# Late input's statistics and normalising moved behind chunk masks, feed-forward steps placed between the products of an inversion, and one reload issued later

## What is computed

```
x = x + 0.5 * _L0_ffn_ref(_layernorm(x), gate, up, down)
x = x + _L0_attn_ref(_layernorm(x), ...)      # causal convs, gated delta-rule recurrence, 16 heads
x = x + 0.5 * _L0_ffn_ref(_layernorm(x), gate, up, down)
x = x + 0.5 * _L1_ffn_ref(_layernorm(x), W_r, W_k, W_v, mu_r, mu_k)
x = x + _L1_attn_ref(_layernorm(x), Wqkv, Wout)   # softmax inside blocks of 64
x = x + 0.5 * _L1_ffn_ref(_layernorm(x), W_r, W_k, W_v, mu_r, mu_k)
```

## Time and profile before

| | us |
|---|---|
| median of three runs | 8338.34 |
| lowest and highest | 8326.64, 8341.58 |
| span of the profiled execution | 8338.4 |
| PE busy | 6513.2 (78%) |
| DVE busy | 4672.6 (56%) |
| ACT busy | 2618.7 (31%) |
| POOL busy | 2154.0 (26%) |
| mean share of the full TensorE clock that was granted | 0.886 |

### The profile page before, as it was taken

The page is one execution under the profiler, slowest core; times in us unless marked ns, Lnnn a source line. Parts: engine busy times, 40 slices in busy tenths (PEclk is TensorE's granted clock), DMA queues, the critical chain, the costliest instruction groups (busy, mean ns, idle before and its releaser), DMA issues. The chain is left out here.

```text
span 8338.4 us, 162585 instructions
## 1 busy us (share of the span) xinstructions
PE 6513.2 (78%) x60160; PEld 4694.8 (56%) x60160; DVE 4672.6 (56%) x10226; ACT 2618.7 (31%) x5275; POOL 2154.0 (26%) x3555
## 2 busy tenths in 40 slices
PE   6787787877878788787877878778787787878776
PEld 4555646556565565655556465565655656556564
DVE  6556564554655546565464655546555465654653
ACT  3223242332423224242242423324233242422421
POOL 1413223041321413214032230413204132140321
PEclk9898898988989899898888989889888988988887
DMA  1100011001100110001100010010101110010000
GB/s 52 24 34 20 26 29 32 26 20 36 27 23 26 29 37 20 21 31 24 37 20 26 29 32 26 20 36 27 24 26 25 40 20 21 31 24 37 20 26 3
DMA packets 376529, 226.31 MB, mean 27 GB/s; under 512 B 336896, under 2 KB 353920, under 8 KB 367488
## 3 DMA queue, kind: packets, MB, share of 16 engines
q1 hardware_dynamic: 375680, 215.29, 9.4%
HBM read 156.54 MB, written 58.72 MB: 26 GB/s over the span
## 5 line engine op out<-in xcount | busy, mean ns | idle before, releaser
L806 DVE SCALAR_TENSOR_TENSOR PS<-SC,CW,PS 128x512 f32<-128x512 f32 x1536 | 1155.2, 753 | 157.7 <-DVEq L804 79.4
L1525 PE MATMUL PS<-CST,SC 128*128 128x128 f32 x2512 | 452.3, 322 | 462.9 <-PEq L1580 290.5
L1028 POOL TENSOR_TENSOR RSTD<-VAR,NHALF 128x2 f32<-128x2 f32 x202 | 143.2, 709 | 2124.3 <-POOLq L1027 1995.9
L1525 PEld LDWEIGHTS PS<-CST,SC 128*128 128x128 f32 x2512 | 334.0, 164 | 578.2 <-issue 561.9
L1187 POOL TENSOR_TENSOR FR<-MS,NHALF 128x8 f32<-128x8 f32 x128 | 210.0, 1641 | 1564.5 <-POOLq L1186 1297.4
L1522 PE MATMUL PS<-XT,WV 128*128 128x512 f32 x1024 | 537.7, 653 | 58.1 <-PEq L1827 58.1
L1111 POOL TENSOR_TENSOR WO<-WO 128x30 f32<-128x30 f32 (+14 forms) x960 | 517.9, 539 | 136.5
L1522 PE MATMUL PS<-XT,WQK 128*128 128x512 f32 x1024 | 534.6, 658 | 0.0
L1108 POOL TENSOR_TENSOR WO<-WO 128x30 f32<-128x30 f32 (+14 forms) x960 | 475.4, 495 | 119.9 <-issue 6.9
L1522 PEld LDWEIGHTS PS<-CST,SC 64*64 64x64 f32 (+1 forms) x4224 | 346.7, 180 | 243.8 <-issue 243.0
L1522 PE MATMUL PS<-SC 128*64 128x32 f32 (+1 forms) x3264 | 269.3, 302 | 271.7 <-PEq L1650 199.5
(11 more groups left out here) (158 smaller groups left out, 12600.3 us busy)
## 6 DMA issues: line engine op xcount, KB each, us to landing
WV<-in_wv SPq DMA_DIRECT2D x16, 2048.0 KB, 7.4
WO<-in_wo SPq DMA_DIRECT2D x16, 2048.0 KB, 7.5
WQK<-in_wq SPq DMA_DIRECT2D x16, 1024.0 KB, 4.8
WQK<-in_wk SPq DMA_DIRECT2D x16, 1024.0 KB, 7.3
cells_in<-SC SPq DMA_DIRECT2D x128, 128.0 KB, 3.3
WO<-cells_in SPq DMA_DIRECT2D x32, 512.0 KB, 3.4
cells_out<-WO SPq DMA_DIRECT2D x32, 512.0 KB, 2.6
cells_nat<-WO SPq DMA_DIRECT2D x32, 512.0 KB, 3.6
```

The lines of the kernel that those rows point to most:

```text
L806: op = v.scalar_tensor_tensor(y, pre[:, j:j + G], CW[:, i * TAPS + j:i * TAPS + j + 1], y, ALU.mult, ALU.add)
L1028: q.tensor_tensor(out=RSTD[:, 2 * k:2 * k + 2], in0=VAR[:, 2 * k:2 * k + 2], in1=NHALF[:, 0:2], op=ALU.pow).then_inc(rstd_ready, 1)
L1525: return nc.tensor.matmul(out_, in_, ident, is_transpose=True, start=True, stop=True)
```

## The change

It has three parts; no computation is added or dropped.

- DVE: `late_stats` and `late_normal` are gone. `stats(0)` and `stats(1)` stand behind the masks of chunks 1 and 2, `normal(0)` and `normal(1)` behind the masks of chunks 4 and 5. POOL's two `rstd` of these stand at chunks 1 and 2 and no longer at chunk 7.
- PE and ACT: two of the ten steps that stood ahead of the inversion's products (g12 and g13) stand between them: g12 after `inverse_q`, g13 after `inverse_t`. PE's wait for `d_back` so comes two steps earlier in its program. DVE and POOL keep their ten steps in a row.
- SP: the scatter of the first half is issued ahead of the reload of `M`.

```diff
                 gather(1)
                 spill()
+                scatter(0)
                 sp.dma_start(M, cells_in[1]).then_inc(m_loaded, 16)
-                scatter(0)
                 spill()
...
                     if 0 <= c < CHUNKS:
                         masks(c)
-                    if i == CONV_TILES - 3:
-                        late_stats(late)
-                    if i == CONV_TILES - 2:
-                        late_normal(late)
+                    if c in (1, 2):
+                        stats(c - 1, late)
+                    if c in (4, 5):
+                        normal(c - 4, late, LXN, txn_ready)
...
-                    if c == CHUNKS - 1:
-                        rstd(0)
-                        rstd(1)
+                    if c in (1, 2):
+                        rstd(c - 1)
                     if c >= HALF:
                         substitute(5 * (c - HALF) + 1, 5 * (c - HALF) + 6)
...
-                fill(FILL_FIRST)
+                fill(FILL_FIRST - 2)
                 for y in range(2):
                     inverse_q(y, bank(2 + y))
+                fill(1)
                 for y in range(2):
                     inverse_t(0, y, bank(2 + y))
+                fill(1)
...
-                fill(FILL_FIRST - 1)
+                fill(FILL_FIRST - 3)
                 pe.wait_ge(d_back, 96)
                 pe.sem_inc(d_back, -96)
                 for y in range(2):
                     inverse_q(0, y, bank(2 + y))
+                fill(1)
                 pe.wait_ge(qp_ready, 2)
                 pe.sem_inc(qp_ready, -2)
                 for y in range(2):
                     inverse_t(0, y, bank(2 + y))
+                fill(1)
                 pe.wait_ge(ti_ready, 2)
                 pe.sem_inc(ti_ready, -2)
                 keys_t(0)
```

## The result

The changed kernel takes **8210.97 us** (median of four runs, 8203.00 to 8218.35), against 8339.96 for the kernel before on the same chip (8326.64 to 8344.84): a ratio of 0.9847, with a 95% interval of 0.9835 to 0.9858. The forecast was 8207, its range 8160 to 8275. A group is 498.4 us long on average in place of 506.6, 8.2 less.

What follows compares the result with a forecast made beforehand. No engine is always busy; PE, ACT, POOL and DVE wait for each other in turn. Per group 4.2 + 3.0 + 0.6 - 0.3, plus 0.7 for the clock, is 8.2; times 16, 131 us off 8338.4 gives 8207, range 8160 to 8275.

Steps and rivals of the forecast that it cites:

- End of the projections: DVE's late statistics and normalising leave the projections' end: g01 starts 4.2 us earlier a group, ends 4.0 and 4.4.
- POOL and the scatter: POOL no longer waits for statistics at chunk 7: spill 5.72 us earlier, scatter issued in 2.29, landing 1269.2 not 1276.7.
- The steps between the products: At the inversion, g12 and g13 cover both copy waits: 3.0 us a group; `keys_t` starts 7.4 us earlier.
- Chunk loop: Statistics and normalising pieces fit DVE's 1.39 us idle behind the masks; cost 0.3 us a group.
- Clock: Granted clock at second product, keys and what follows may stay at the upper level: 0.7 us a group taken.
- (a): Rival: clock stays up through the inversion's products, 2.3 us a group in place of 0.7: 8181; chance 0.13.
- (b): Rival: chunk loop pays the whole 5.3 us, leaving 2.9 a group: 8292; chance 0.15 with partial forms.
- (c): Rival: POOL finds another wait, scatter still lands at 1276.7, nothing gained: 8338; chance 0.07.
- (d): Rival: scatter not earlier, PE waits 8.8 us, clock falls, two steps cost 3.6+0.1 more a group: 8398; chance 0.05.

Runs made afterwards that it cites:

- norm34: Changed kernel with the two halves of the normalising behind the masks of chunks 3 and 4 in place of 4 and 5: 8222.10 us, ratio 0.9857.
- fill: The part that moves two steps between the inversion's products on PE and ACT; alone, against the kernel before, 8345.88 us, ratio 1.0002.
- late: Kernel before with only the late input's four pieces and POOL's two powers moved into the chunk loop: 8268.86 us, ratio 0.9910.
- fill_only: Kernel before with only the two steps moved between the products on PE and ACT: 8345.88 us, ratio 1.0002.
- pad_22: Changed kernel with five extra products in each group ahead of the first feed-forward's down projections, result unused: 8279.91 us, ratio 0.9922.
- sp_only: Kernel before with only the reload of M issued behind the scatter: 8311.44 us, ratio 0.9961.

## Why the prediction was right

The total was right to 4 us, and the saving per group too, 8.2 of 8.2. Its terms were less so: the end of the projections gave 1.2 less than its 4.2, the clock at least 0.9 more than its 0.7, and the two errors went against each other.

- **End of the projections.** Forecast 4.2, with ends 4.0 and 4.4; measured 3.6 in the third group and 3.0 on average. The step "the taps of tile 31 need ACT's scaling" held, and DVE does wait 0.88 for it. What was mis-sized is ACT: I had it hold up the tanh by up to 0.4. DVE now waits 0.79 for the tanh, and PE, with the normalised rows already transposed, stands 2.52 at L1807 for the value copy. The late engine there is now ACT, and my ends were too narrow.
- **POOL and the scatter.** Spill forecast 5.72 earlier, measured 5.4. The issue of four DMAs forecast at 2.29, measured 2.29. Last issue ended at 1266.3-1053.4 = 212.9 by the forecast, at 213.1 in the trace. The wait at `d_back` was forecast at 1.3, measured 0.99; it occurs in 11 of 16 groups, 9.6 us in all. This was the best part of the working, and every price in it was a row's.
- **The steps between the products.** Both copy waits went, as forecast (3.0 a group). `keys_t` was to come 7.4 earlier and came 5.7 earlier in the third group, 6.3 on average. Of the 1.7 missing in the third group 0.3 is the start of the first product (216.1 where the sum has 215.8); the late g01 doesn't count, since PE waited for the scatter in any case. The rest lies in the four pieces behind it: the first product took 4.92 for 4.12, g12 3.71 for 1.81, the second product 2.15 for 3.63, g13 1.92 for 1.81. So the stall and the lower level in g12 cost 2.7, and the second product at a higher level gave back 1.5. The stall was in the row 1277.28 x70 before, and I took the whole 4.12 of the first product, 1.67 of stall in it, as its length.
- **Chunk loop.** Forecast 0.3 a group, measured 0.35+0.19 in every second group, 0.27. The size of these two is right and half of their reason is wrong. At chunk 5 the normalising did take 1.46 beside POOL, 0.73 beside nothing: an operation held for as long as POOL's. By the Trainium skill's rule of an exclusive lock (SBUF — State Buffer, "SBUF: two separate sides") it could be late by up to 0.5. The trace has 0.73 more for the two operations and 0.19 for the chunk; in norm34, which took POOL from their side, they took 0.73 again. But the larger share, 0.35 at chunk 4, is DVE's wait for `gam_ready` (0.71), not its own work. And as a whole the loop became 0.2 shorter, since chunk 7 is no longer late in five groups, which I had not in the sum.
- **Clock.** I took 0.7, between nothing and 2.3. Behind the first key alone it gave 1.57 in a group, and the experiments tie that to `fill`; so this term was too small. Ahead of the keys both ends occur: the ninth group runs through at 1.00 and the third is at 0.62 and 0.50. So the condition of rival (a), no fall between the products, is met in six of the sixteen groups. In the second and third the clock was at 0.50 behind time in which PE stood (1.38 us at L2031 in the second; 0.99 there and the first 0.2 of the stall in the third), so the waits of the copies were not needed for it. The Trainium skill's rule (TensorE: Matmul & The Clock Gate, Part 1), that the throttled state is the default and activity releases it, agrees: 32x32 products with steps between them kept 1.00. But the time of (a), 8181, didn't come, and an early key is no short group: the ninth group starts its keys at 226.7 and is 494.9 long, the third at 228.8 and 498.3, but the fifteenth at 226.3 and 498.3, and the second at 227.9 and 494.9.
- **What I missed** is that a group's length moves in steps. The sum of terms, 8.2, is met on average, since 15 groups fall on different steps. The saving ahead of the keys is 6.3, and 1.57 of the 1.9 behind them is the clock at the keys and chunk 0. That the total fits to 4 us is in part luck: `late` alone fell 22 us below its sum, and extra work of 55 us cost 100.
- **The other rivals.** (b) fell: 0.27 in place of 5.3 a group. (c) fell with the spill. (d) fell twice: the landing was early, and fill_only, where it was late, lost nothing in all, though its g12 did run at the lower level.

## What to carry to other kernels

Work that fills a wait pays only when what the next wait is for comes earlier too: the steps between the products were worth nothing alone, nothing with the late input, and 49 us with both other parts. So test parts together as well as alone before one is thrown out. When a dependent small transfer and a large one that nobody awaits stand in one queue, issue the small one first; it cost a line and brought 0.4% alone, nothing with the late input, and 0.6% with both other parts. And read how a kernel's time answers to a few microseconds added, before trusting a sum to less than one of its steps. In a kernel that repeats itself, look where the granted clock rises in each repetition.

## What the runs showed of the hardware

- PE stands still up to 3.1 us (norm34, pad_22; 2.6 in the changed kernel) inside its work, with nothing in the profile that it waits for. The places are fixed in its instruction stream, return every fourth group, and move when 24 products are added far ahead of them. In all it is 6.6 us (sp_only) to 27.0 (pad_22) of a run.
- The lower clock level costs short stretches dearly: g12 took 3.7 us from its start to the second product's at 0.50 (third group), against 1.92 at 1.00 (ninth). The clock fell after PE had stood for 1.38 us, or for 0.99 and then 0.2; it kept 1.00 through waits of 0.93 and 1.10 in two other groups.
- From the first key to the end of the 28 products behind it PE took 4.0 us in the four kernels with copy waits ahead of the keys, and 2.4 to 2.5 in the three where steps fill them.
- Issuing the same four DMAs took 3.75 us behind a 512 KB reload and 2.29 ahead of it.
- The length of a group changes in steps of about 3.4 us, in all kernels measured; 3.5 us of extra PE time changed one group by three steps and the next by none. In all of them the granted clock rises from 0.50 to 1.00 between 7.15 and 7.42 us ahead of the first product of twelve groups of the sixteen. Why the clock rises when it does is open.
